# Gate and down products of two pages alternated expert by expert in a mixture-of-experts page loop

## The reference, cut to what matters

```python
x = x + conv_ref(ln_c(x), ...)
t = to_tokens(x)                                  # 16384 x 64
probs = softmax(ln_t(t) @ gate_w + gate_b)        # 16 experts
top_probs, top_idx = top_k(probs, 2)              # two experts per token
h1 = ln_t(t) @ w1[e]; h2 = ln_t(t) @ w2[e]        # 64 -> 128, per expert
expert_out = (silu(h1) * h2) @ w3[e]              # 128 -> 64
t = t + sum over e of expert_out * dispatch[e]
```

## Time and profile before

| | us |
|---|---|
| three runs | 543.36, 538.32, 542.36 |
| median | 542.36 |
| profiled execution, device time | 534.76 |
| its span, first to last instruction | 531.4 |
| PE busy | 474.5 (89%) |
| DVE busy | 397.2 (75%) |
| POOL busy | 284.7 (54%) |
| ACT busy | 257.0 (48%) |

### The profile page before, as it was taken

The page is one execution under the profiler, slowest core; times in us unless marked ns, Lnnn a source line. Parts: engine busy times, 40 slices in busy tenths (PEclk is TensorE's granted clock), DMA queues, the critical chain, the costliest instruction groups (busy, mean ns, idle before and its releaser), DMA issues.

```text
span 531.4 us, 15123 instructions
## 1 busy us (share of the span) xinstructions
PE 474.5 (89%) x4774; PEld 415.7 (78%) x4774; DVE 397.2 (75%) x913; ACT 257.0 (48%) x461; POOL 284.7 (54%) x378
## 2 busy tenths in 40 slices
PE   6888989898997678589998999999999999999992
PEld 5566667675774478579998999999989999999981
DVE  5557787988888778898776777776877768777682
ACT  4667788885873553134443443434444344443420
POOL 4000007777777775757777755454444444445552
PEclk9789899998987859699999999999999999999996
DMA  6981012020200244201203432133333525211034
GB/s 253 340 153 41 0 41 66 26 66 28 68 30 28 51 95 86 48 25 42 60 25 82 88 72 46 45 62 88 85 92 88 132 46 136 55 41 53 23 125 158
DMA packets 62664, 41.02 MB, mean 77 GB/s; under 512 B 50004, under 2 KB 54319, under 8 KB 62081
## 3 DMA queue, kind: packets, MB, share of 16 engines
q1 hardware_dynamic: 52208, 23.84, 20.1%
q0 software_dynamic: 8800, 8.94, 5.2%
q10 hardware_dynamic: 1584, 7.29, 3.5%
HBM read 21.46 MB, written 19.19 MB: 76 GB/s over the span
## 4 chain that ended last, share of the span: by engine, by line
PE 67%; DVE 14%; issue 7%; POOL 6%; ACT 3%; DMA 2%; SPq 1%; POOLq 0%; DVEq 0%; ACTq 0%
PE turn L962 21%; PE up L947 10%; PE up L948 10%; PE up L771 8%; PE small L788 4%; PE small L817 3%; POOL results L510 3%; POOL pages L522 3%; PE small L856 3%; PE up L746 2%; PE turn L800 2%; ACT rstd_wide L586 1%; DVE up_w L1166 1%; PE lines L969 1%; PE turn L861 1%
## 5 line engine op out<-in xcount | busy, mean ns | idle before, releaser
L510 POOL DMA_INDIRECT results<-result,page_in x147 | 145.7, 991 | 119.8 <-ACT xc L701 89.7
L522 POOL DMA_INDIRECT pages<-payload,slot_int x128 | 132.9, 1038 | 110.5 <-DVE slot_int L1376 73.3
L701 ACT ACTIVATE xc<-up,gate_unscale 128x512 f32<-128x512 f32 x147 | 101.1, 688 | 180.0 <-PE up L948 160.7
L947 PE MATMUL up<-xs_hi,up_w 128*128 128x128 f16 x1176 | 149.9, 221 | 6.2 <-DVE sq L1555 3.3
L948 PE MATMUL up<-xs_lo,up_w 128*128 128x128 f16 x1176 | 149.8, 221 | 0.0
L947 PEld LDWEIGHTS up<-xs_hi,up_w 128*128 x1176 | 123.9, 105 | 6.9 <-issue 6.8
L948 PEld LDWEIGHTS up<-xs_lo,up_w 128*128 x1176 | 116.5, 99 | 0.1
L1555 DVE SCALAR_TENSOR_TENSOR hidden<-up,hidden_scale,xc 128x512 f32<-128x512 f32 x74 | 55.5, 750 | 39.1 <-ACT xc L701 36.8
L962 PE MATMUL turn<-down_raw,sq 128*128 x584 | 79.5, 279 | 1.4 <-issue 0.4
L962 PE MATMUL turn<-down_raw,hidden 128*128 x592 | 78.5, 276 | 1.6 <-issue 0.4
L962 PEld LDWEIGHTS turn<-down_raw,sq 128*128 128x128 f32 x584 | 70.8, 191 | 9.5 <-issue 6.9
(11 more groups left out here) (238 smaller groups left out, 605.2 us busy)
## 6 DMA issues: line engine op xcount, KB each, us to landing
pages<-x ACTq DMA_DIRECT2D x4, 1332.0 KB, 10.4
page_in<-pages SPq DMA_DIRECT2D x147, 36.0 KB
page_in<-pages SPq DMA_DIRECT2D x147, 32.0 KB
x_in<-in_x SPq DMA_DIRECT2D x7, 512.0 KB, 3.5
out<-up_raw SPq DMA_DIRECT2D x5, 512.0 KB, 2.8
results<-result,page_in POOLq DMA_INDIRECT x147
up_raw<-in_L_ffn_w SPq DMA_DIRECT2D x4, 512.0 KB, 17.8
pages<-payload,slot_int POOLq DMA_INDIRECT x128, 2.2
```

Of the source, the lines that this page charges most:

```text
L510: pool.indirect_dma_start(out=results, out_offset=bass.IndirectOffsetOnAxis(ap=page_in[g % LOADS][:, k, D + AT_TOKEN:D + AT_TOKEN + 1].bit ...
L522: pool.indirect_dma_start(out=pages, out_offset=bass.IndirectOffsetOnAxis(ap=slot_int[q % PAYLOADS][:, t:t + 1], axis=0), in_=payload[q % ...
L701: act.activation(act_s[n % 2], up[n % 2][:, 0:CW], ACT.Silu, scale=gate_unscale[:, 0:1])\
L947: pe.matmul(target, own, xs_hi[g % 2][:, at], start=True, stop=False)
```

## The change

Three things are changed. `LAG` becomes 2. On PE, `products(n)` takes the place of `up_product(n)` and `down_product(n - LAG)`: all waits stand ahead of it, then for each of the four places a gate product of page n and a down product of page n - 2 follow each other, then come the four value products of page n. The transposes of the next group, the roster load and `turn_back` follow behind. The up weights `up_w` stand 256 float16 numbers apart instead of 128, half of it unused. DVE's, ACT's, POOL's and SP's code is the same but for `LAG`, which is in the condition for `weigh`.

```diff
-    LAG = 3
+    LAG = 2
...
-        up_w = [sb(f"up_w{m}", [P, E, HID], F16) for m in range(2)]
+        up_w = [sb(f"up_w{m}", [P, E, 2 * HID], F16) for m in range(2)]
...
+            def up_product(n, m, j, e):
+                g, k = n // BY, n % BY
                 at = slice(k * P, (k + 1) * P)
...
+                target = up[n % 2][:, m * CW + j * P:m * CW + (j + 1) * P]
+                own = weights[m][:, bass.ds(e * (2 * HID // STRIDE), HID)]
+                pe.matmul(target, own, xs_hi[g % 2][:, at], start=True, stop=False)
+                return pe.matmul(target, own, xs_lo[g % 2][:, at], start=False, stop=True)
...
+            def products(n):
+                g, k, d = n // BY, n % BY, n - LAG
+                if n < PAGES:
+                    if k == 0:
+                        pe.wait_ge(xs_ready, g + 1)
+                    if n >= 2:
+                        pe.wait_ge(hidden_done, n - 1)
+                else:
+                    pe.wait_ge(hidden_done, d + 1)
+                if 0 <= d and d % 2 == 0:
+                    if d < 4:
+                        pe.wait_ge(channels_ready[d // 2], PAIRS)
+                    else:
+                        pe.wait_ge(weighed_done, d // 2 - 1)
+                for j in range(PER_LINE):
+                    if n < PAGES:
+                        gates = up_product(n, 0, j, experts[n][j])
+                        if j == PER_LINE - 1:
+                            gates.then_inc(gates_ready, 1)
+                    if d >= 0:
+                        down = down_product(d, j, experts[d][j])
+                        if j == PER_LINE - 1:
+                            down.then_inc(down_done, 1)
+                if n < PAGES:
+                    for j in range(PER_LINE):
+                        values = up_product(n, 1, j, experts[n][j])
+                    values.then_inc(up_ready, 1)
...
-                if n < PAGES:
-                    up_product(n, experts[n])
+                products(n)
...
-                if 0 <= n - LAG < PAGES:
-                    down_product(n - LAG, experts.pop(n - LAG))
```

More of the change, by code:

```diff
@@ L645, in make_hi @@
                 act.wait_ge(weights_made, WM_SCALES)
-                act.activation(up_w[m][:, :, :], up_raw[:, m, :, :], ACT.Copy, scale=scales[:, m:m + 1])\
+                act.activation(up_w[m][:, :, 0:HID], up_raw[:, m, :, :], ACT.Copy, scale=scales[:, m:m + 1])\
                     .then_inc(hi_made, 1)
@@ L933, in experts_of @@
                 return values
-            def up_product(n, experts):
+            weights = [w[:, :, :].rearrange("p e h -> p (e h)") for w in up_w]
+            whole = down_raw[:, :, :].rearrange("p e d -> p (e d)")
+            def up_product(n, m, j, e):
                 g, k = n // BY, n % BY
[L937 to L941, removed]
-                at = slice(k * P, (k + 1) * P)
[L943 to L949, removed]
@@ L951, in down_product @@
-            def down_product(n, experts):
-                m, k = n // 2, n % 2
[L953 to L963, removed]
+                at = slice(k * P, (k + 1) * P)
@@ new lines, in up_product, with down_product @@
+                target = up[n % 2][:, m * CW + j * P:m * CW + (j + 1) * P]
+                own = weights[m][:, bass.ds(e * (2 * HID // STRIDE), HID)]
+                pe.matmul(target, own, xs_hi[g % 2][:, at], start=True, stop=False)
+                return pe.matmul(target, own, xs_lo[g % 2][:, at], start=False, stop=True)
+            def down_product(n, j, e):
+                m, k = n // 2, n % 2
+                return pe.matmul(turn[m % 2][:, (k * PER_LINE + j) * D:(k * PER_LINE + j + 1) * D],
+                                 hidden[n % RING][:, j * P:(j + 1) * P], whole[:, bass.ds(e, D)], start=True, stop=True)
@@ L984, in _ @@
                     rank(RANK[n])
-                if n < PAGES:
-                    up_product(n, experts[n])
+                products(n)
+                experts.pop(n - LAG, None)
                 if n % BY == 0 and n // BY + 1 < GROUPS:
@@ L1165, in make_low @@
                 dve.wait_ge(hi_made, 2 - m)
-                dve.scalar_tensor_tensor(out=up_w[m][D:P, :, :], in0=up_raw[D:P, m, :, :], scalar=scales[D:P, m:m + 1],
-                                         in1=up_w[m][D:P, :, :], op0=ALU.mult, op1=ALU.subtract).then_inc(lo_made, 1)
+                dve.scalar_tensor_tensor(out=up_w[m][D:P, :, 0:HID], in0=up_raw[D:P, m, :, :], scalar=scales[D:P, m:m + 1],
+                                         in1=up_w[m][D:P, :, 0:HID], op0=ALU.mult, op1=ALU.subtract).then_inc(lo_made, 1)
             links = 0
```

## The result

The changed kernel took 547.74 us, median of 20 runs (540.91 to 554.98); the kernel before took 539.00 beside it, median of 20 (532.52 to 545.26). The ratio is 1.0137, with an interval of 1.0103 to 1.0171: **slower by 7.4 us (5.6 to 9.2)**. The ratio compares the faster runs of both kernels, while the medians take in slower ones at a lower mean clock; of the profiled executions, that of the kernel before (534.76) is a fast one, those of the changed kernel (550.26, and 550.75 when it ran again) are slow ones. The forecast was +12 us, 554. Its direction held; its size did not.

A forecast was written before the change was run, and what follows sets the result against it. PE bounds the page loop, with DVE a quarter free; DVE would set the changed round. 9.5 + 2.2 + 1 = 12.7, taken as +12 on the 542.36 median: 554 us, likeliest 548 to 561, 8 in 10 543 to 567.

The forecast's parts named there:

- The mechanism: Page loop: later gates and DVE's work between two hides make PE wait at page 4k+4, about 0.5 us a group.
- The second rival: Page loop: float32 loads lie under float16 matmuls, 0.28 an expert, or DVE's burst runs 0.4 shorter; 542 us; chance 0.17.
- the first: Rival, page loop: alternation loses 0.11 at each of seven float16 to float32 steps, 24 us on top, 578 us; chance 0.10.
- the wake: From the end of a DVE hide to PE's next matmul at page 4k+4: 0.26 us.
- The turn-backs: Ten in the page loop: five at pages 4k+2 cost nothing, five at pages 4k cost 0.44 each, +2.2 us.
- 8.60 for DVE's round: From PE's first gate matmul of page 4k to page 4k+4: 8.60 us against 8.30, +9.5 us over 31.5 groups.
- hide of 4k+1 to hide of 4k+2: On DVE: 3.21 us, from 2.54 for the earlier longer stretch plus 0.67 for xs_lo.
- the term: Pages 20 to 146: 9.5 us for DVE setting the group's end plus 2.2 for turning back, +11.7 us.
- Register steps, counted as 0: On PE: four plain register steps a page replace four of the other kind, hidden because PE does not wait for them; 0.
- The third rival: PE's issue gap at the roster load is covered, PE's group falls to about 7.7; 523 or 530 us; chance 0.08.
- The stage before page 20: DVE's long jobs restart with gates 0.68 later, an earlier down product gives back some 0.9; +1 us, ends -2 and +4.
- The end, counted as 0: After page 146: the order is the same and the end follows its silu; 0.

## Why the forecast missed

**What held.** The mechanism: the page that ends the round, the operations that make it, and the wait it ends in, are the ones named. Per expert 0.333 us where 0.337 was forecast. Silu 1.34 behind its page's first matmul (345.33 against 343.99), forecast 1.3. PE waits at pages 4k, 0.5 us. The second rival needed 0.28 an expert and is out as a matter of load times; the first needed an extra 0.11 at each change of type and is out by the same 0.333. A burst 0.4 shorter was the other way to the second rival's time; it was 0.16 shorter, with 0.07 from the wake, and the result lies between that rival's time and the forecast. The turn-backs came as forecast: the groups that begin with pages 80, 96, 112 and 128 take 8.82 to 8.86 from silu to silu, the other full groups ahead of page 140 take 8.38 to 8.48, and those at pages 4k+2 cost nothing.

The Trainium skill ("TensorE: Matmul & The Clock Gate", section "The mechanism") also has a sentence that loads overlap running matmuls only where their row groups differ. All loads here fill the same 128x128; by that sentence the float32 loads gain nothing from the float16 matmuls ahead of them, and the 0.333 agrees, where the general rule of the section cited in the prediction does not. The float16 loads do not fit it: they last 0.10 each and follow one another every 0.056 in this trace while their matmuls run. Why a float32 load is not hidden stays open.

**The step that failed: 8.60 for DVE's round.** Measured are 348.54 - 340.15 = 8.39, and 33.62 / 4 = 8.41 over pages 20 to 36. Along the steps of the prediction:

| step | forecast | measured |
|---|---|---|
| hide of 4k to hide of 4k+1 | 2.24 | 342.39 - 340.15 = 2.24 |
| hide of 4k+1 to hide of 4k+2 | 3.21 | 345.44 - 342.39 = **3.05** |
| hide's end to PE's first product | 0.26 | 346.38 - 346.19 = **0.19** |

The other two steps of the round came out as priced: hide itself 0.75, and from PE's first product to hide 348.54 - 346.38 = 2.16 where 2.14 was used. Inside the 3.05 the steps are 0.66, 0.72, 0.73, 0.34 and 0.60. The priced ones were 0.74, 0.73, 0.72, 0.35 and 0.67. The first, 0.74, was 347.06 to 347.80 in the earlier trace rows, and that row was not a burst: the weighing there waited for its down products, whose last matmul ended at 346.67 + 1.10 = 347.77, in this row of PE's timeline of the kernel before.

```profile
346.67 1.10 PE L962 MATMUL turn<-down_raw,sq 128*128 x8
```

The last, 0.67, is nearly xs_lo's own duration, 0.68, taken where the operation behind it needs nothing from it. In these rows an operation of DVE whose inputs are ready starts 0.07 to 0.09 before the one ahead ends (0.75 long, 0.66 to the next; 0.68 and 0.60; 0.42 and 0.34, with xs_lo early 0.35), one that reads the result of the one ahead 0.04 behind its end (0.68 and 0.72, 0.69 and 0.73). Both pairs could be seen in the earlier trace rows: 0.43 long and 0.35 to the next is the first kind, and I used it for one step only. The wake of 0.26 came from the one hide waited for in the earlier trace rows, where the mean clock is 0.76; in this stretch it is 0.19.

The 0.19 to 0.21 a group that these make, times 31.5 groups, are 6.0 to 6.6 us of the 7.1 by which the term was too large (11.7 against 4.6). As the forecast was a difference of 0.30 between 8.60 and 8.30, an error of 2.5% in the first removed two thirds of it. The rest is in the turn-backs and the last pages: the fifth turn-back, at page 144, is in the half group at the end, where no next group is transposed. Of the 6.3 us by which 554 was above the median, 3.4 have nothing to do with the change: the three runs that the forecast started from had a median of 542.36, the twenty beside the change 539.00.

**Register steps, counted as 0.** That "PE does not wait for them" in the gapless page of the earlier trace rows did not make them free: they go with 4.4 us when the stride alone is changed. In the changed kernel this gain is hidden behind DVE's round, and it returns wherever that is short, as in the 253.98 of late weighing. Where ACT writes the weights the stride cost nothing: 1.99 us each in the changed kernel too. The third rival was therefore half right: PE's gaps do shrink, to 4 x 1.988 = 7.95 a group, but only in a kernel in which DVE's round is shorter than that.

**The stage before page 20: +1, with ends of -2 and +4.** Measured +5.8, outside both ends, and gone with the old order up to page 20 (56.9, 56.6 and 56.9 in three kernels). Most of it, 2.7 and 2.3 us, falls behind DVE's long jobs at pages 6 and 11. Silu of page 7 to silu of page 8 took 220.33 - 210.22 = 10.1 before and takes 12.8:

```profile
217.74 0.69 ACT L701 ACTIVATE xc<-up,gate_unscale 128x512 f32<-128x512 f32 x1 [1.10 <-PE up L944]
230.53 0.69 ACT L701 ACTIVATE xc<-up,gate_unscale 128x512 f32<-128x512 f32 x1 [3.01 <-PE up L944]
```

The lag alone makes it 11.6, and so does the change with the old order there (11.6): 1.4 to 1.5 us for the weighing and adding that now stand ahead of the long job, and 1.2 more once the alternating order is there too. Over their whole first stage the lag alone (57.0) and the change with the old order (56.6) make these 1.5 up again, so what stays lost goes with the alternating order. In the window behind that job, 222 to 236 us, the mean granted clock is 0.54; in the kernel before, 214 to 228 us, it is 0.63. The second job is followed by a second fall. Of each kernel the window behind page 11; first the change, then the change with the old order up to page 20 (the third figure from the end is PE's clock):

```profile
245.00:255.00 10.00, 9.92 (x88) 9.93 (x89) 6.74 (x13) 2.06 (x3) 6.87 (x7) 0.66 0.07 23
```

```profile
240.00:250.00 10.00, 9.96 (x127) 9.62 (x126) 8.05 (x17) 3.92 (x6) 7.29 (x8) 1.00 0.08 27
```

PE is busy all through both, and does 88 matmuls at a mean of 0.66 against 127 at 1.00: much of this restart runs at 1.2 GHz, not at 2.4. Pages 12 to 16 take 13.1 us in place of 10.7. The alternating order is not enough for that: with xs_lo early and with the alternation at the old lag it stands from page 0 on too, but the clock did not fall behind page 11 and the stage took 58.7 and 57.2 us; with late weighing it fell (a mean of 0.72 from 238 to 250 us), and the stage took 60.2. That the clock falls in some and not in others is seen; that the late gates make it fall is argued from the order of events. And both profiled executions of the changed kernel, the sources of the +5.8, have that second fall; whether its other runs have it is not shown.

**The end, counted as 0**, is 1.2 us shorter (19.6 to 18.4). It is 18.1 to 18.5 in all kernels with LAG = 2 and early weighing (the lag alone among them) and 19.6 to 20.0 in the others, so it goes with the last weighing, which is issued a page earlier. My sum let the end "follow its silu" and left out what follows.

**What stays open**: the total of the change with the old order up to page 20, which its stages do not explain, and the 2 us by which the stages of the profiled executions (+9.2) exceed the middle of the measured difference (+7.4), at the edge of its interval. Runs of the changed kernel without the second fall of the clock could explain these 2 us, but none was profiled. What sets the landing of page 40's loads is open too.

## What to carry to other kernels

Where a forecast is the small difference of two long rounds, price each step of the new round from a row in which its neighbour is of the same kind (ready, or reading the result just made) and not from a row that ended on another engine's wait: 0.2 us of 8.6 was two thirds of the forecast effect here. When two edits both lengthen one chain, look for the operation on it that has slack elsewhere; moving xs_lo ahead of a hide that waits anyway turned the change from 1.4% slower into 1.2% faster. And cut a loop into its stages before calling a term small: in the profiled executions the 20 pages in which DVE is the busier engine lost more than the 126 behind them.

## What the runs showed of the hardware

The time that PE's instruction stream spends on register steps seems to count even where PE shows next to no idle time (39.67 of 40 us busy before): where each of four steps a page took 8 ns less, a page was 0.031 us shorter (2.040 to 2.009) and pages 20 to 146 4.4 us (126 x 0.032 would be 4.0); with late weighing, at either stride, it was 0.029 (2.017 to 1.988).

In the rows here DVE starts an operation ahead of the end of the one before it, by 0.07 to 0.09 us, unless it reads what that one writes; then it starts 0.04 behind that end.

Float16 and float32 products in turn took the sum of their own steps: two float16 steps of 0.056 and two float32 steps of 0.112 are 0.336, and an expert took 0.333.
